# A packed attention layer: projections moved to every second step, unread products moved ahead of the scores

## The reference

```
h   = layernorm(x) * (1 + scale) + shift
q, k, v = split(h @ W_qkv + b_qkv)                  # self-attention
x   = x + gate * (softmax(q k^T / sqrt(8)) v @ W_proj + b_proj)
q   = layernorm(x) @ W_q + b_q ; k, v = split(ctx @ W_kv + b_kv)
x   = x + softmax(q k^T / sqrt(8)) v @ W_co + b_co  # cross-attention, 77 keys
x   = x + gate_m * mlp(layernorm(x) * (1 + scale_m) + shift_m)
```

## Time and profile before

| | us |
|---|---|
| median of 3 runs | 3427.48 (3426.73 to 3434.89) |
| the profiled execution | 3441.14, its span 3439.3 |
| PE busy | 3029.5 (88%) |
| DVE busy | 2612.0 (76%) |
| ACT busy | 2246.9 (65%) |
| mean granted clock of PE | 0.946 of full speed |
| layer 1's attention, first scores | at 1443.3 |
| layer 2's attention, last scores | at 2901.7 |

### The profile page before, as it was taken

One profiled execution on the slowest core, in us unless ns is written; L12 is line 12 of the kernel. 1 busy time (PEld: TensorE's weight loads), 2 busy tenths in 40 slices (PEclk: granted clock), 3 DMA queues, 4 the chain that ended last, 5 costly groups with the idle time before them and its releaser, 6 DMA issues. The chain is left out here.

```text
span 3439.3 us, 93774 instructions
## 1 busy us (share of the span) xinstructions
PE 3029.5 (88%) x31851; PEld 2015.6 (59%) x31851; DVE 2612.0 (76%) x12300; ACT 2246.9 (65%) x5561; POOL 1041.2 (30%) x1278
## 2 busy tenths in 40 slices
PE   5999977777777779799999998989999999889998
PEld 3544444444444457566666665556666666558887
DVE  4878769999999978588887764568887775546665
ACT  2666657777777657367776666647776666646665
POOL 0000046666666656511122211121112221112221
PEclk9999969999989989899999999979999999989999
DMA  1111000000000000144444430034444442000000
GB/s 44 45 51 35 18 10 9 9 9 9 8 8 9 4 1 1 46 102 105 106 107 102 104 96 5 1 92 105 104 106 103 103 103 56 1 32 16 21 21 18
DMA packets 145007, 165.37 MB, mean 48 GB/s; under 512 B 41494, under 2 KB 93974, under 8 KB 144278
## 3 DMA queue, kind: packets, MB, share of 16 engines
q1 hardware_dynamic: 132374, 133.32, 15.4%
q0 software_dynamic: 12160, 26.04, 3.2%
HBM read 18.85 MB, written 4.19 MB: 7 GB/s over the span
## 5 line engine op out<-in xcount | busy, mean ns | idle before, releaser
L1374 ACT ACTIVATE attn_pT<-attn_t 128x512 f32<-128x512 f32 (+1 forms) x1024 | 555.4, 596 | 321.7 <-PE attn_t L1631 321.7
L1491 DVE TENSOR_REDUCE attn_mx<-attn_s 128x4 f32<-128x512 f32 (+1 forms) x1024 | 549.2, 578 | 142.0 <-PE attn_s L1616 141.2
L1616 PEld LDWEIGHTS attn_s<-packed_keys,packed_queries 32*128 32x128 f32 x4096 | 277.3, 190 | 163.6 <-DVE attn_mx L1491 95.6
L659 ACT ACTIVATE topk_prob<-topk_s,topk_nmx 128x77 f32<-128x77 f32 x1024 | 248.3, 326 | 181.8 <-DVE topk_work L840 160.5
L1616 PE MATMUL attn_s<-packed_keys,packed_queries 32*128 32x128 f32 (+1 forms) x4096 | 342.2, 288 | 14.8 <-DVE attn_mx L1491 7.2
L1289 POOL DMA_DIRECT2D packed_queries<-attn_om x256 | 142.8, 558 | 649.3 <-ACT attn_om L1367 645.5
L1023 PE MATMUL topk_s<-kbd,topk_qT 128*128 128x308 f32 x512 | 216.3, 507 | 129.8 <-ACT topk_prob L659 129.5
L1656 PE MATMUL attn_o<-attn_pT,attn_vp 128*18 128x128 f32 (+1 forms) x8192 | 327.1, 278 | 0.0
L503 POOL TENSOR_SCALAR topk_mask<-topk_work 128x308 f32<-128x308 f32 x256 | 250.1, 977 | 239.8 <-DVE topk_work L845 238.6
L1631 PE MATMUL attn_t<-packed_queries,packed_keys 32*128 32x128 f32 (+1 forms) x4096 | 300.4, 264 | 0.0
L1631 PEld LDWEIGHTS attn_t<-packed_queries,packed_keys 32*128 32x128 f32 (+1 forms) x4096 | 227.9, 166 | 4.7 <-ACT attn_pT L1374 3.4
(11 more groups left out here) (328 smaller groups left out, 7543.0 us busy)
## 6 DMA issues: line engine op xcount, KB each, us to landing
packed_queries<-attn_qT SPq DMA_DIRECT2D x720, 64.0 KB, 2.2
packed_keys<-attn_kT SPq DMA_DIRECT2D x384, 64.0 KB, 2.1
packed_queries<-attn_om POOLq DMA_DIRECT2D x256, 64.0 KB, 2.3
packed_queries<-zero_rows SPq DMA_DIRECT2D x120, 128.0 KB, 2.7
packed_keys<-attn_kT SPq DMA_DIRECT2D x384, 39.0 KB, 2.3
kbd<-window_kT SPq DMA_DIRECT2D x512, 8.0 KB
kbd<-topk_kT SPq DMA_DIRECT2D x512, 4.8 KB
x_res<-in_x SPq DMA_DIRECT2D x16, 192.0 KB, 2.6
```

Of the source, the lines that this page charges most:

```text
L659: last = nc.scalar.activation(prob[:, n % NP, h * keys:(h + 1) * keys], s_ps[:, u % 2, h * keys:(h + 1) * keys], ACT.Exp, scale=SCALE, bia ...
L1374: nc.scalar.activation(pT[0:keys, c % 2, h, :], t_ps[0:keys, h, :], ACT.Exp, scale=SCALE).then_inc(s_exp, 1)
L1491: nc.vector.tensor_reduce(mx[:, (c // 2) % 2, 2 * k + h, :], sc, AX.X, ALU.max).then_inc(s_max, 1)
L1616: last = nc.tensor.matmul(s_ps[:, h, k * KW:(k + 1) * KW], r.qp[32 * j:32 * j + 32, buf, k, b * T:(b + 1) * T], r.kp[32 * j:32 * j + 32, b ...
```

## The change

The preparation of a group is spread to steps two apart, the values move into step 0 of the next iteration, and the unread products move ahead of the scores and into the scores' bank:

- The turned rows move from step 3 to 2, keys from 5 to 4, queries stay in 6. Values of group i + 2 were projected in step 7 of iteration i; now those of group i + 1 are in step 0 of iteration i.
- `UNREAD` gets eight entries, 3 in step 1 and 2 in steps 3, 5 and 7: again 9 per iteration. `keep_clock` is now called between `scores_waits` and the scores, writes `s_ps[:, 0, :]`, and has no wait of its own. In iterations 30 and 31 all eight steps have two. Behind the last scores it still issues two per step.
- On DVE the statistics are all in step 2, the variance in 3, and the normalised rows in steps 5 and 7. `low_keys` and `low_queries` follow KP and QP; the values are copied out in step 0.
- On ACT `modulate`, `keys_out` and `queries_out` follow XT, KP and QP (steps 2 and 3, 4, 6).
- On POOL the context columns for group i + 2 are fetched in step 1, where those of group i + 3 were in step 7. SP's order of transfers is unchanged.

```diff
-    XT, KP, QP, VP = 3, 5, 6, 7
+    XT, KP, QP, VP = 2, 4, 6, 0
     ONT, PROJ = 2, 4
-    UNREAD = (2, 3, 2, 2)
+    UNREAD = (0, 3, 0, 2, 0, 2, 0, 2)
...
-                    if u == VP and NG <= i + 3 < NT:
-                        stage_context(i + 3)
+                    if u == 1 and NG <= i + 2 < NT:
+                        stage_context(i + 2)
...
                         if u == 2:
-                            ln_stats(i + 3, (0, 1, 2))
+                            ln_stats(i + 3)
                         if u == 3:
-                            ln_stats(i + 3, (3,))
                             ln_variance(i + 3)
-                        if u == XT + 1:
+                        if u == 5:
                             ln_apply(i + 3, (0, 1))
-                    if u == 0 and i > 0 and there(before, left, 2):
-                        ln_apply(i + 2, (2, 3))
+                        if u == 7:
+                            ln_apply(i + 3, (2, 3))
...
-                        if u == VP:
-                            values_out(i + 2, (m3 + 2) % 3)
+                    if u == VP and i > 0 and there(before, left, 1):
+                        values_out(i + 1, (m3 + 1) % 3)
...
-            def keep_clock(g, buf, count):
-                pe.wait_ge(s_v, min(g + 2, NT))
+            def keep_clock(buf, count):
                 for _ in range(count):
-                    nc.tensor.matmul(l_ps[:, :], r.kp[:, buf, 0, 0:T], r.kp[:, buf, 0, :], start=True, stop=True)
+                    nc.tensor.matmul(s_ps[:, 0, :], r.kp[:, buf, 0, 0:T], r.kp[:, buf, 0, :], start=True, stop=True)
...
                     if now:
                         scores_waits(i, u)
+                        keep_clock(m3, UNREAD[u] if there(before, left, 2) else 2)
+                    elif back:
+                        after(pe, s_max, 2 * NS * NT)
+                        keep_clock((m3 + dg) % 3, 2)
...
-                    if now and u < len(UNREAD):
-                        keep_clock(i, m3, UNREAD[u])
-                    elif not there(before, left, 2) and (now or back):
-                        keep_clock(i, m3, 2)
...
-                        if u == VP:
-                            project_values(i + 2)
+                    if u == VP and i > 0 and there(before, left, 1):
+                        project_values(i + 1)
```

## The result

| | before | after |
|---|---|---|
| median | 3429.93 us (4 runs, 3426.73 to 3434.89) | 3608.19 us (4 runs, 3605.28 to 3613.46) |
| the profiled execution, its span | 3441.14, 3439.3 | 3609.43, 3607.6 |

The ratio is 1.0505, 95% interval 1.0475 to 1.0534: the change makes the kernel 178 us slower. The forecast was 3551 us with a range of 3500 to 3655; the sign and the range held, and the size was 57 us short.

A forecast was written before the change was run, and what follows sets the result against it. Each step was bound by its ring or PE's own work; +2.12 us per iteration gave +119 us for 56, plus 5 for the last iterations: 3441.14 to 3565, less 14 for the median, 3551 us, range 3500 to 3655.

The forecast's parts named there:

- The ring of the odd steps: In odd steps the next scores wait for maxima (self-attention, 2.11 us) or exponentials (cross-attention, 1.96 us), a floor per step.
- PE's own work in even steps: In self-attention, PE's matrix work sets steps 0, 2, 4 and 6: 2.97, 2.50, 3.53 and 2.44 us.
- The unread products in the open: Nine per iteration, ahead of the odd steps' scores, covered by nothing: 2.67 us per iteration.
- The wait that goes: Before the queries' projection, PE's 1.05 us wait for DVE to read out the keys disappears.
- The sum for undisturbed iterations: Self-attention 22.55 us, cross-attention 21.57, mean 22.06 against 19.94: +2.12 per iteration, +119 us for 56.
- rival B: The clock falls behind odd steps' empty ends; one fall per iteration costs 56 to 140 us: 3607 to 3691; chance 0.20.
- A: The forecast itself with its terms off, 3505 to 3590 us; chance 0.61.
- The profiled execution and the median: The median of the runs was taken as 13.7 us below the profiled execution, turning 3565 into 3551 us.
- The ends: Iterations 30 and 31 add 5 us for both layers; iterations 0 and 1 add 0, 5 either way per layer.
- the tails' 5: In iterations 30 and 31, unread pairs ahead of scores cost about 0.3 in five of eight steps: +5 us, both layers.
- Rival C: Unread products cost only 0.23 us each behind the wait, 2.07 and not 2.67 per iteration: 3517 us; chance 0.08.
- Rival D: Unread products run while PE would wait anyway, and the removed wait is a plain gain: 3372 us; chance 0.05.

The follow-up runs named there:

- e1: The changed kernel with no unread products in iterations 0 to 29; 3480.58 us, ratio 1.0146 to the kernel before.
- e2: The changed kernel with one more unread product ahead of each odd step's scores (4, 3, 3, 3); 3637.09 us, ratio 1.0603 to before.
- e4: The changed kernel with the same nine unread products behind the odd steps' scores and values' products; 3428.20 us, ratio 1.0009 to before.
- e3: The kernel before with its own steps, only its unread products moved ahead of the scores; 3588.76 us, ratio 1.0457 to before.
- e6: The changed kernel with preparation on odd steps, outputs a step later, no unread products in iterations 0 to 29; 3583.14 us, ratio 1.0436 to before.
- e7: e6 with one unread product in each of steps 0 and 2; 3577.22 us, ratio 1.0427 to before.
- e11: e7 with four of the transfers that pack a group's queries issued by POOL instead of SP; 3385.62 us, ratio 0.9837 to before.

## Why the prediction was right, and where it was short

- **The ring of the odd steps** held: 2.11 us in self-attention, three of the four odd steps. The fourth, step 7, took 2.27 (1666.14 to 1668.41): its successor waits for packed keys. That is 0.16 more than forecast.
- **PE's own work in even steps**, less the unread pair of 0.66: step 2 is 2.52 (forecast 2.50), step 4 3.29 (3.53), step 6 2.44 (2.44), and step 0, which lasts 3.86 with three unread products of 0.89, 2.97 (2.97). Only the keys were put too high, by 0.24; that their projection overlaps its neighbours more there was not tested.
- **The unread products in the open**, forecast 2.67 per iteration, measured 2.88 (e1). Each pair took 0.66 and not 0.60. That they stand on the chain is shown from both sides by e1 and e2, and e4 shows that the same nine cost nothing in another place.
- **The wait that goes**: it went, and gained little, as e3 against after shows: with the wait and unspread steps 22.75 and without it 22.68 in self-attention. In cross-attention the steps without the wait are the longer ones, 21.35 against 20.67: the even steps have no room there for the work that came to them. (With the unread products out of the way, in e4, an iteration is 0.27 and 0.3 us shorter than before.)
- **The sum for undisturbed iterations** was right: 22.55 forecast and 22.68 measured, 21.57 and 21.35. Some of that is luck, since errors of opposite sign cancel: in self-attention +0.16 and +0.21 against -0.24, and between the kinds +0.13 against -0.22. With the four lengths between the kinds, the mean of 27 undisturbed periods is (12 x 22.68 + 22.52 + 21.98 + 21.76 + 21.73 + 11 x 21.35) / 27 = 22.04, +2.10 against the 19.94 before, where I had +2.12.
- **The step that failed** is the weight of rival B. I gave the falling clock its own 0.20 and put nothing of it in the forecast. The 18 falls lengthened 14 of the 54 periods, fewer than the third that I had named inside A at 3580. The mean of all periods is 22.72, so the clock took (22.72 - 22.04) x 54 = 37 us. The place was right as well: cross-attention, behind an idle end of a step of about 0.6 us. My argument against it, that self-attention stood still 1.05 us per iteration at full clock, held for self-attention (2 falls), and I had carried it over to cross-attention.
- **The profiled execution and the median** lay 13.7 us apart before, and I took the same for after. There it was 1.2 us, which is 12 of the 57 us that the forecast fell short; 37 are the clock, 9 the ends, and the iterations give 1 back.
- **The ends** were put too low: outside the 54 periods the span grew by 168.3 - 150.1 = 18 us, where two more iterations at +2.12 and the tails' 5 make 9. From the last keys of layer 1 to the first of layer 2 after needs 213.8 us, before 202.4; with the unread products behind (e4: 2018.15 to 2226.46) it is 208.3. So the place of the unread products is about half of the excess; the rest I did not test.
- **Rival C** (0.23 each) had the right spacing and the wrong sum. A further product costs 0.23 (e2), near the 216 ns that the Trainium skill, "TensorE: Matmul & The Clock Gate", section "Back-to-back issue gap", gives as the isolated gap for 512 columns; the 131 ns that it gives for a stream of weight loads and products is not seen here. But the first of a burst costs about 0.43 (0.66 - 0.23), so nine in four bursts cost 2.88 and not 2.07.
- **Rival D** (faster) falls as argued: the even steps last 2.44 to 3.29 us without their pair, longer than the maxima. It needed the unread products behind the scores of the odd steps, and e4 did just that.

In sum, of the 168 us between the profiles, (22.04 - 19.94) x 54 = 113 are undisturbed iterations, 37 the clock and 18 the rest.

## What to carry to other kernels

Filler work on the busiest engine is free only in time that the engine would wait anyway: put it behind the product that others wait for, not ahead of it. Evening out stages means counting each step against its ring: without unread products a self-attention iteration took 19.80 us with the preparation in the steps that don't end in a wait (e1), and 18.35 us with it in those that do, its outputs taken a step later (e6). And when a faster schedule comes out slower, look for the first still stand ahead of each fall of the clock: in e6 and e7 it was a transfer queue, full at 18.5 us per iteration, and four transfers on another queue turned a kernel 4% slower than before into one 1.6% faster. That kernel differs from before in the steps, the place and number of the unread products and the queues at once; from e7 it differs in the queues alone.

## What the runs showed of the hardware

- The cost of a short still stand of PE depends on what follows. In after the 0.5 us or so at the end of a step were mostly followed by nothing, often by a short fall, which cost 1.6 us (22.93 to 23.01 in place of 21.35), and in two iterations by some 17 us at the lower level, which cost 7.2 and 7.4 us. In e6 a still stand of 2.5 us was followed by tens of us at the lower level (0.50 from 2026 us on), though PE then counted as busy throughout: at 1.2 GHz the same iteration took 28.6 us and not 17.1, its engine full.
- A mean granted clock says little by itself: e11 has 0.927 and before 0.946, and e11 is 47 us faster.
- Two kernels with the same shortest iterations (e7 and e11, both 18.7 us in self-attention and 17.6 in cross-attention) differ by 192 us in their runs. The shortest iteration was no guide to the time; how many reached it was.
- Transfers issued back to back by one engine's queue took about 0.7 us each (26 in 18.5 us), keys of 64 and of 39 KB alike (e6: 8.17 us for twelve from 1577.23, 8.24 us from 2003.77).
